# First attention: inputs and normalised outputs turned in 32x32 squares on VectorE instead of by TensorE

## The chip, the cores and the metric

One core of one Trainium2 chip runs the whole program. The metric is the device time in microseconds. The kernel before takes 1017.32 us, the median of three runs (1017.08 to 1018.11).

## The reference, cut to what matters

Two layers. Layer 0: causal attention with 16 heads of 16 columns on 4 x 512 x 256 inputs, rotary turn of the first 4 columns, output projection; then the residual and a layer normalisation; then a "wave" part that gates, mixes and normalises. Layer 1: linear attention and six MLP blocks. The kernel works in fp32, split into a high and a low part for TensorE (`x = x_h + x_l`, three products for one). The change touches layer 0's attention and what hands its result on:

```python
qkv = jnp.einsum('bsh,hf->bsf', hidden_states, w_qkv) + b_qkv
...
scores = jnp.einsum('bhqd,bhkd->bhqk', q, k)
scores = jnp.where(causal, scores, jnp.float32(-jnp.inf).astype(scores.dtype))
probs = jax.nn.softmax(scores, axis=-1)
attn = jnp.einsum('bhqk,bhkd->bhqd', probs, v)
...
return jnp.einsum('bsh,hf->bsf', attn, w_out) + b_out
```

Three things must be turned (token rows to columns) for a product over the hidden dimension: the input of each batch for the projection to q, k and v ("x_T"), the attention's outputs for the output projection ("att_T"), and the normalised rows for the gates of the wave part ("next_T").

## The kernel before, in words

`attention0` handles one batch per entry: `entry(0, "first")`, two of kind "loop", `entry(3, "last")`. An entry has 8 pairs of heads (p) with 4 tiles (r) each: 32 slots (p, r). All engines run the same list of slots, each its own queue in order, tied by semaphores. A slot on TensorE is a score product of two heads (`score_pass`, L849), a product for the row maxima of the pair after next (`max_pass`, L838), often a value product (`value_pass`, L862), and one use of PSUM bank 5 ("work") from the table `WORK_AT`: "stack" (turn the stacked heads, L892), "project" (L885), "out" (L901), and the three kinds of turn (`x_T`, `att_T`, `next_T`, all at L957: four transposes of 128 x 128 for one half c of the columns). Work for batch i+1 (x_T, stack, project) and for batch i-1 (att_T, out, next_T) is woven into entry i. The fourth batch's outputs and normalised rows are turned behind the entries.

ScalarE computes the exponentials (L710), copies PSUM to the heads (`copy_k` L697, `copy_q` L703), rounds the stack (`stack_high`, L689, L691), copies the outputs (L742) and rounds each turned half to its high part (`high`: L678 for x_T, L680 att_T, L682 next_T). VectorE takes the maxima (L1126), the rows of maxima (L1140), adds biases, subtracts the low parts of the turned halves (`low`, L1163), and normalises (`layernorm_steps`, two small steps in each slot from (4, 0) on; the last of them, L167, writes xn at (5, 1)). GpSimd masks the diagonal (`select`, L594), turns by the rotary angles (`rotate`), subtracts the low parts of the stack (L600, L602), adds biases to the residual (L621) and keeps rows (L614). SyncE moves the rows of maxima (`max_row`, L530, two DMAs) and loads each batch's input (L538) as soon as x_T of the one before is split. The score product of slot (p, 0) waits for the row of maxima of its pair; each score product waits for the first exponential of the slot before; each max product for VectorE's maxima of the slot before; a value product for the mask of two slots before. Some filler products (`keep_busy`, L966) stand at (0, 2) and at the places of `KEEP_AT`.

Behind the entries the first waits of the next part are in `gate_product` (L1427, four for each batch) and `gate_function` (L1435). The last stage of the program already turns its rows by squares (L2566, L1687).

Of the kernel before, what the change touches and what calls it, by code (L numbers as in the profile page):

```python
# [25 lines left out]
P = 128  # L26
# [172 lines left out]
def build(nc, A, out):  # L199
# [3 lines left out]
    with top:  # L203
# [78 lines left out]
WORK_AT = ((0, 0, "stack", (1, 0)), (0, 1, "x_T", 0), (0, 2, "stack", (1, 1)),  # L282
           (1, 0, "stack", (1, 2)), (1, 1, "x_T", 1), (1, 3, "stack", (1, 3)),
# [4 lines left out]
           (6, 0, "project", (3, 0)), (6, 1, "project", (3, 1)), (6, 2, "next_T", 0),  # L288
           (7, 0, "project", (3, 2)), (7, 1, "next_T", 1), (7, 3, "project", (3, 3)))
# [14 lines left out]
PREVIOUS = ("att_T", "out", "next_T")  # L304

LOW_FIRST = ((0, 2), (2, 1))
# [13 lines left out]
def work_table(when):  # L320

    table = {}
    for p, r, kind, arg in WORK_AT:
        if kind in PREVIOUS:
            used = when != "first"
        else:
            used = when != "last" if kind == "x_T" else of_entry(when, arg[0])
        if used:
            table[p, r] = (kind, arg)
# [46 lines left out]
def attention0(nc, A, g, top):  # L376
# [21 lines left out]
    s = g.first = sems(top, nc, "ident_in rope_in const_in first_T first_p first_v first_s first_copied qkv_in0 qkv_in1 out_in wsplit_h wsplit_l g_wout const_v mask_v x_in xres_in g_res g_ones "  # L398
# [3 lines left out]
             "v_bias v_matrix a_split v_split a_gate_h v_gate_l p_gate a_gate p_tail v_tail a_c")  # L402
    wqkv_h = put(nc, "wqkv_h", g.early, 0, [KC, 3 * D], F32R)
# [78 lines left out]
    def _(sp):  # L482
# [68 lines left out]

        max_row(-1, "before", 0)
        entries(sp, entry)

    @block.gpsimd
    def _(pool):
# [60 lines left out]

        def residual_bias(b, t):
# [6 lines left out]
        def entry(i, when):  # L625
            table = work_table(when)
            for p in range(PAIRS):
                for r in range(RT):
                    if (p, r) in LOW_AT and of_entry(when, LOW_AT[p, r][0]):
                        stack_low(i, *LOW_AT[p, r])  # L630
                    select(i, p, r)
                    kind, arg = table.get((p, r), (None, None))
# [25 lines left out]
        entries(pool, entry)  # L658
        for t in range(RT):
            keep(B - 1, t)  # L660

    @block.scalar
    def _(act):
# [10 lines left out]
        def high(i, when, kind, arg):  # L674

            act.wait_ge(s["p_work"], WORK.number(i, when, (kind, arg)))
            if kind == "x_T":
                act.activation(x_h[:, arg, :], work, ACT.Copy).then_inc(s["a_xT"], 1)  # L678
            elif kind == "att_T":
                act.activation(att_h[:, arg, :], work, ACT.Copy).then_inc(s["a_attT"], 1)  # L680
            else:
# [2150 lines left out]
```

## Time and profile before

| | |
|---|---|
| median of three runs | 1017.32 us |
| profiled execution, its time | 1017.09 us |
| span of its trace | 1015.0 us |
| mean granted TensorE clock | 0.991 |
| prologue of the first attention | 0 to 28.5 us |
| entries of the first attention | 28.5 to 298 us |
| gates and wave part | 298 to about 430 us |
| busy over the span: TensorE, VectorE, ScalarE, GpSimd | 96%, 75%, 60%, 35% |

PE is TensorE's matmul queue, PEld its weight loads, DVE VectorE, ACT ScalarE, POOL GpSimd, SP SyncE. The chain of work that ended last goes mostly through TensorE's products of the last stage; the change is made long before these. A row of the timeline has the start in us, the duration in us, engine, line, operation, output and inputs with their shapes, and a count where like instructions are merged; in brackets is the idle time before it and what ended that.

### The profile page before, as it was taken

The numbers are of one execution on the slowest core, as the hardware profiler recorded it, in microseconds if no ns is written. First come the engines' busy times: TensorE is split into PE (matmuls) and PEld (weight loads), VectorE is DVE, ScalarE is ACT, GpSimd is POOL, SyncE is SP. The second block draws the span as 40 slices with busy tenths as digits, with TensorE's granted clock in tenths as the row PEclk, the third lists the DMA queues.
The fourth block names the chain that finished last, engine by engine and source line by source line (L and its number), as shares of the span: only waits on it lengthen the run. The fifth ranks groups of instructions, "written<-read, shape, count | busy, mean of one in ns | idle before, by whom it ended". The sixth has DMA issues, their size and how long they took to land.

```text
span 1015.0 us, 18314 instructions
## 1 busy us (share of the span) xinstructions
PE 970.5 (96%) x6498; PEld 806.6 (79%) x6498; DVE 756.8 (75%) x2083; ACT 609.3 (60%) x1177; POOL 360.3 (35%) x646
## 2 busy tenths in 40 slices
PE   8899999998989898999999999999999999999997
PEld 6555555555758798787899999999999999999897
DVE  6677787866656778967767787888778788687874
ACT  5566667655358774645745566665566665566660
POOL 5454374552131374443832222223222232222410
PEclk9999999998999999999999999999999999999999
DMA  7000000013020001032010221220112022121201
GB/s 260 22 2 22 2 23 22 24 43 104 22 89 1 4 2 42 1 104 63 32 53 23 73 67 27 63 64 26 52 45 67 22 64 63 32 62 33 62 32 54
DMA packets 54834, 47.41 MB, mean 47 GB/s; under 512 B 6900, under 2 KB 52184, under 8 KB 54744
## 3 DMA queue, kind: packets, MB, share of 16 engines
q1 hardware_dynamic: 50328, 41.65, 13.5%
q10 hardware_dynamic: 4416, 4.59, 1.5%
q8 instruction: 52, 0.85, 0.4%
q14 instruction: 38, 0.31, 0.1%
HBM read 31.40 MB, written 4.20 MB: 35 GB/s over the span
## 4 chain that ended last, share of the span: by engine, by line
PE 54%; DVE 5%; POOL 2%; issue 1%; ACT 1%; DVEq 0%; POOLq 0%; ACTq 0%
PE ps L1970 24%; PE ps L1987 24%; PE ps L1868 2%; DVE ln_stats L2388 1%; PE ps L2000 1%; PE ps L1919 1%; POOL hs L1765 1%; DVE xT_l L2522 0%; POOL x_b L1765 0%; PE ps L1882 0%; DVE amp L2424 0%; PE ps L1897 0%; DVE G_l L2528 0%; PE ps L1910 0%; POOL x_a L1795 0%
## 5 line engine op out<-in xcount | busy, mean ns | idle before, releaser
L2224 ACT ACTIVATE G<-ps,bias_col 128x512 f32<-128x512 f32 x192 | 135.7, 707 | 156.5 <-PE ps L1970 148.1
L1987 PE MATMUL ps<-w_l,G_h 128*128 128x256 f32 x736 | 203.8, 277 | 0.0
L1987 PE MATMUL ps<-w_h,G_l 128*128 128x256 f32 x736 | 203.8, 277 | 0.0
L1987 PE MATMUL ps<-w_h,G_h 128*128 128x256 f32 x736 | 203.7, 277 | 0.0
L2528 DVE TENSOR_TENSOR G_l<-G,G_h 128x512 fp32r<-128x512 f32 x192 | 164.2, 856 | 48.2 <-ACT G_h L2225 48.2
L1795 POOL TENSOR_TENSOR x_a<-xn,mlp_g 128x1024 f32<-128x1024 f32 x20 | 56.2, 2811 | 326.5 <-DVE xn L2554 326.5
L710 ACT ACTIVATE probs<-ps 128x512 f32<-128x512 f32 (+3 forms) x256 | 98.3, 441 | 97.1 <-PE ps L849 96.3
L1970 PE MATMUL ps<-xT_h,w_h 128*128 128x512 f32 x384 | 150.3, 391 | 0.7 <-DVE xT_l L2522 0.4
L1970 PE MATMUL ps<-xT_h,w_l 128*128 128x512 f32 x384 | 149.6, 390 | 0.0
L1970 PE MATMUL ps<-xT_l,w_h 128*128 128x512 f32 x384 | 149.5, 389 | 0.0
L1126 DVE CUSTOM_DVE_ANT_0 ps<-ps,q_mask 128x128 f32<-128x128 f32 (+3 forms) x256 | 120.7, 512 | 28.7 <-PE ps L838 28.3
L1987 PEld LDWEIGHTS ps<-w_h,G_h 128*128 128x128 f32 x736 | 138.4, 188 | 0.9
L1987 PEld LDWEIGHTS ps<-w_l,G_h 128*128 128x128 f32 x736 | 138.2, 188 | 1.0
L1987 PEld LDWEIGHTS ps<-w_h,G_l 128*128 128x128 f32 x736 | 138.2, 188 | 0.0
L2225 ACT ACTIVATE G_h<-ps,bias_col 128x512 fp32r<-128x512 f32 x192 | 135.3, 705 | 0.0
L594 POOL TENSOR_SCALAR_AFFINE_SELECT probs<-probs 128x256 f32<-128x256 f32 x128 | 53.0, 415 | 99.0 <-ACT probs L710 98.3
L1970 PEld LDWEIGHTS ps<-xT_h,w_h 128*128 128x128 f32 x384 | 72.1, 188 | 15.3 <-issue 0.6
L1970 PEld LDWEIGHTS ps<-xT_h,w_l 128*128 128x128 f32 x384 | 72.1, 188 | 15.2
L1970 PEld LDWEIGHTS ps<-xT_l,w_h 128*128 128x128 f32 x384 | 72.1, 188 | 14.1
L2542 DVE TENSOR_TENSOR rsum<-ps,x_a 128x1024 f32<-128x1024 f32 x23 | 28.2, 1225 | 68.3 <-PE ps L1987 68.3
L838 PE MATMUL ps<-heads_T 64*128 64x128 f32 (+3 forms) x256 | 56.0, 350 | 5.9 <-DVE top_score L1126 5.8
L849 PE MATMUL ps<-heads_T 64*128 64x512 f32 (+3 forms) x256 | 54.3, 419 | 5.2 <-ACT probs L710 3.0
(329 smaller groups left out, 2101.3 us busy)
## 6 DMA issues: line engine op xcount, KB each, us to landing
w_raw<-L_ffn_W_T SPq DMA_DIRECT2D x12, 1024.0 KB, 5.4
landed<-squares SPq DMA_DIRECT2D x320, 32.0 KB, 1.9
hs<-L_attn_hidden_states SPq DMA_DIRECT2D x8, 512.0 KB, 3.9
x_kept<-hs SPq DMA_DIRECT2D x4, 512.0 KB, 4.3
w_raw<-x_kept SPq DMA_DIRECT2D x2, 1024.0 KB, 6.0
out<-xn SPq DMA_DIRECT2D x3, 512.0 KB, 2.8
w_raw<-L_ffn_ent_w_T SPq DMA_DIRECT2D x1, 1024.0 KB, 9.1
w_raw<-L_ffn_ent_pw SPq DMA_DIRECT2D x1, 1024.0 KB, 11.3
```

Of the source, the lines that this page charges most:

```text
L594: pool.affine_select(diagonal, diagonal, [[0, 2], [1, P]], ALU.is_ge, 0.0, base=0, channel_multiplier=-1).then_inc(s["g_sel"], 1)
L710: act.activation(probs[:, p % 2, o, OFF[j]:OFF[j] + COLS[j]], ps[:, score_bank(r, o), 0:COLS[j]], ACT.Exp).then_inc(s["a_exp"], 1)
L838: pe.matmul(ps[:, o, 0:(t + 1) * P], heads_T[rows, p // UP, 0, p % UP, t * P:(t + 1) * P], heads_T[rows, p // UP, 1, p % UP, 0:(t + 1) * P ...
L849: pe.matmul(ps[:, score_bank(r, o), 0:COLS[j]], heads_T[rows, p // UP, 1, p % UP, j * P:(j + 1) * P], heads_T[rows, p // UP, 0, p % UP, j ...
L1126: v.tensor_tensor_reduce(ps[:, o, 0:(t + 1) * P], ps[:, o, 0:(t + 1) * P], q_mask[:, S - (t + 1) * P:S], 1.0, MASKED, ALU.add, ALU.max, to ...
L1795: pool.tensor_tensor(g.x_a[:, rows, :], xn[:, b % 2, :, :], bcast(g.mlp_g[:, i, :], 1, [P, RT, D]), ALU.mult).then_inc(feed["g_mul"], 1)
L1970: mm = pe.matmul(ps[:, hidden_bank(i, n), :], w[:, c, f * P:(f + 1) * P], x[:, b, c, :], start=(k == 0), stop=(k == 5))
L1987: mm = pe.matmul(ps[:, 4 + t // 2, (t % 2) * D:(t % 2 + 1) * D], x[b % 2][f][:, t * P:(t + 1) * P], w2_chunk(w, f), start=(k == 0), stop=( ...
L2224: act.activation(G32[n % 4], bank, ACT.Gelu, bias=bias)
L2225: act.activation(G_h[b % 2][f], bank, ACT.Gelu, bias=bias).then_inc(feed["a_g"], 1)
L2528: v.tensor_tensor(G_l[b % 2][f], G32[n % 4], G_h[b % 2][f].bitcast(F32), ALU.subtract).then_inc(feed["v_gl"], 1)
L2542: v.tensor_tensor(g.rsum[:, :, :], ps[:, 4:6, :].rearrange("p a (b c) -> p (a b) c", c=D), g.x_a[:, b * RT:(b + 1) * RT, :], ALU.add).then ...
```

## The change

Inputs. Each batch is loaded in four quarters of 32 partitions (`load_squares`), so laid out that VectorE's transpose of 32 x 32 squares (`x_turn`, four instructions of 128 x 256 at slots (0, 0), (0, 1), (0, 2), (1, 0)) gives the turned input in SBUF, `x_turned`, which lies in the place of x_l. ScalarE rounds it at (0, 3) and (1, 2), GpSimd subtracts the low part at (1, 0) and (1, 3). The first project product of an entry waits for GpSimd. Batch 0 is turned as before, in the prologue; the load of batch 1 is now issued before the first row of maxima, those of batches 2 and 3 at p = 2 to 5 of entries 0 and 1.

Normalised rows. VectorE transposes the squares of xn behind the normalisation (four instructions of 128 x 256 from slot (5, 2) on, `g.squares`), SyncE moves 16 pieces of squares to `g.landed` at p = 6, 7 and p = 0, 1 of the next entry, ScalarE rounds at (3, 1) and (3, 3) of the entry after that and GpSimd subtracts at (3, 2) and (4, 0). Batch 2's go behind the entries. The first gate product of batches 0 to 2 waits for it. Fillers and all else stay.

```diff
-WORK_AT = ((0, 0, "stack", (1, 0)), (0, 1, "x_T", 0), (0, 2, "stack", (1, 1)),
-           (1, 0, "stack", (1, 2)), (1, 1, "x_T", 1), (1, 3, "stack", (1, 3)),
+WORK_AT = ((0, 0, "stack", (1, 0)), (0, 2, "stack", (1, 1)),
+           (1, 0, "stack", (1, 2)), (1, 3, "stack", (1, 3)),
...
-           (6, 0, "project", (3, 0)), (6, 1, "project", (3, 1)), (6, 2, "next_T", 0),
-           (7, 0, "project", (3, 2)), (7, 1, "next_T", 1), (7, 3, "project", (3, 3)))
+           (6, 0, "project", (3, 0)), (6, 1, "project", (3, 1)),
+           (7, 0, "project", (3, 2)), (7, 3, "project", (3, 3)))
...
-LOW_FIRST = ((0, 2), (2, 1))
+LOW_FIRST = ((2, 1),)
+
+X_TURN_AT = ((0, 0), (0, 1), (0, 2), (1, 0))
+X_HIGH_AT = ((0, 3), (1, 2))
+X_LOW_AT = ((1, 0), (1, 3))
+X_LOAD_AT = (2, 3, 4, 5)
+NEXT_HIGH_AT = ((3, 1), (3, 3))
+NEXT_LOW_AT = ((3, 2), (4, 0))
...
+    SQ, Q = 32, P // 32
+    x_squares = x_in.rearrange("p t d -> p (t d)").rearrange("p (c n r) -> p c n r", c=KC, r=SQ)
+    x_turned = put(nc, "x_turned", g.early, 16 * D, [KC, S // SQ, SQ])
...
         def entry(i, when):
-            if when != "last":
-
-                sp.wait_ge(s["v_xT"], i + 1)
-                sp.dma_start(x_in, x_dram[:, i + 1, :, :]).then_inc(s["x_in"], 16)
             for p in range(PAIRS):
                 if p < PAIRS - 1 or when != "last":
                     max_row(i, when, p + 1)
+                if p in X_LOAD_AT and i + 2 < B:
+                    if p == X_LOAD_AT[0]:
+                        sp.wait_ge(s["v_xturn"], 4 * (i + 1))
+                    load_squares(i + 2, X_LOAD_AT.index(p))
+                if when != "first" and p >= PAIRS - 2:
+                    if p == PAIRS - 2:
+                        sp.wait_ge(s["v_squares"], i)
+                    move_squares(i - 1, p - PAIRS + 2)
+                if i >= 2 and p < 2:
+                    move_squares(i - 2, p + 2)
...
+        def load_squares(b, j):
+
+            rows = A["L0_attn_hidden_states"][b].rearrange("(n t) (c j r) -> j t c n r", t=SQ, c=KC, j=Q)
+            sp.dma_start(x_squares[j * SQ:(j + 1) * SQ, :, :, :], rows[j]).then_inc(s["x_in"], 16)
+
+        def move_squares(b, to):
+
+            for of in range(Q):
+                sp.dma_start(g.landed[to * SQ:(to + 1) * SQ, b, :, :].rearrange("p c (q f t) -> p c q f t", q=RT, f=Q)[:, :, :, of, :],
+                             g.squares[of * SQ:(of + 1) * SQ, b, to, :, :, :]).then_inc(s["moved"], 16)
+
+        sp.wait_ge(s["v_xT"], 1)
+        for j in range(Q):
+            load_squares(1, j)
         max_row(-1, "before", 0)
         entries(sp, entry)
+        for to in (2, 3):
+            move_squares(B - 2, to)
...
+        def x_low(i, c):
+
+            pool.wait_ge(s["a_xT"], KC * (i + 1) + c + 1)
+            pool.tensor_tensor(x_l[:, c, :], x_turned[:, c, :, :].rearrange("p n t -> p (n t)"),
+                               x_h[:, c, :].bitcast(F32), ALU.subtract).then_inc(s["g_xlow"], 1)
+
+        def next_low(b, c):
+
+            pool.wait_ge(s["a_nT"], KC * b + c + 1)
+            pool.tensor_tensor(g.xT_l[:, b, c, :], g.landed[:, b, c, :], g.xT_h[:, b, c, :].bitcast(F32),
+                               ALU.subtract).then_inc(s["g_nlow"], 1)
...
+        def x_high(i, c):
+
+            act.wait_ge(s["v_xturn"], 4 * i + 2 * c + 2)
+            act.activation(x_h[:, c, :], x_turned[:, c, :, :].rearrange("p n t -> p (n t)"), ACT.Copy
+                           ).then_inc(s["a_xT"], 1)
+
+        def next_high(b, c):
+
+            act.wait_ge(s["moved"], 16 * Q * Q * (b + 1))
+            act.activation(g.xT_h[:, b, c, :], g.landed[:, b, c, :], ACT.Copy).then_inc(s["a_nT"], 1)
...
             if kind == "project":
+                if arg == (2, 0):
+                    pe.wait_ge(s["g_xlow"], KC * (i + 1))
                 mm = project(work, *arg)
...
+        def x_turn(i, part):
+
+            if part == 0:
+                v.wait_ge(s["x_in"], 16 + 64 * (i + 1))
+            c, n = part // 2, part % 2 * (S // SQ // 2)
+            v.transpose(x_turned[:, c, n:n + S // SQ // 2, :], x_squares[:, c, n:n + S // SQ // 2, :]
+                        ).then_inc(s["v_xturn"], 1)
...
+            yield
+            v.wait_ge(s["v_norm"], i + 1)
+            for k in range(RT):
+                ins = v.transpose(g.squares[:, i - 1, :, :, k, :].rearrange("p j c s -> p c j s"),
+                                  xn[:, 0, k, :].rearrange("p (c j s) -> p c j s", c=KC, j=Q))
+                if k == RT - 1:
+                    ins.then_inc(s["v_squares"], 1)
+                yield
+                yield
...
@@ -1420,6 +1488,8 @@
     b, w, m = n // 4, n // 2 % 2, n % 2
     if n >= 4:
         pe.wait_ge(g.first["a_gate"], n - 3)
+    if n % 4 == 0 and b < B - 1:
+        pe.wait_ge(g.first["g_nlow"], KC * (b + 1))
```

## Rows read from the trace of the kernel before

**Rows 1.** Busy time in stretches: us, PE, PEld, DVE, ACT, POOL, clock, DMA share, GB/s.

```profile
30.00:298.00 268.00, 247.89 (x1735) 156.10 (x1737) 194.45 (x722) 159.02 (x406) 121.53 (x330) 0.97 0.12 35
200.00:205.00 5.00, 5.00 (x34) 2.87 (x34) 2.11 (x9) 2.21 (x4) 1.68 (x4) 0.66 0.02 3
```

**Rows 2.** Line 957's transposes of inputs and normalised rows: ns min/median/max, first and last start.

```profile
L957 PE MATMUL ps<-ident,hs x24: 272/273/448, 33.8 to 164.4; 128*128 128x128 f32 x24
L957 PE MATMUL ps<-ident,xn x24: 272/273/329, 144.0 to 295.3; 128*128 128x128 f32 x24
```

**Rows 3.** Timeline around slot (0, 1) of the second entry: TensorE, then ScalarE.

```profile
94.42 0.44 PE L849 MATMUL ps<-heads_T 64*128 64x384 f32 x2
...
94.09 0.44 ACT L710 ACTIVATE probs<-ps 128x128 f32<-128x128 f32 x2
```

**Rows 4.** Timeline around slot (6, 2) of the second entry: TensorE, then ScalarE.

```profile
144.05 0.66 PE L957 MATMUL ps<-ident,xn 128*128 128x128 f32 x4
144.63 0.38 PE L849 MATMUL ps<-heads_T 64*128 64x256 f32 x2
...
147.29 0.44 PE L885 MATMUL ps<-wqkv_h,x_h 128*128 128x384 f32 x1 [0.22 <-DVE xT_l L1163]
...
144.56 0.60 ACT L742 ACTIVATE out_T<-ps 128x512 f32<-128x512 f32 x1
145.04 0.62 ACT L682 ACTIVATE xT_h<-ps 128x512 fp32r<-128x512 f32 x1
145.51 0.69 ACT L710 ACTIVATE probs<-ps 128x256 f32<-128x256 f32 x2
```

**Rows 5.** Timeline around slot (7, 1) of the second entry: TensorE, then ScalarE.

```profile
149.85 0.45 PE L849 MATMUL ps<-heads_T 64*128 64x384 f32 x2
...
148.91 0.45 ACT L710 ACTIVATE probs<-ps 128x128 f32<-128x128 f32 x2 [0.97 <-PE ps L849]
```

**Rows 6.** Prices: moves and transposes of squares by tile; GpSimd's timeline; VectorE's groups.

```profile
L1687 SPq DMA_DIRECT2D landed<-squares x320: 585/597/1794, 532.2 to 958.8; - x160
L2566 DVE STREAM_TRANSPOSE squares<-xn x80: 391/416/440, 528.6 to 948.7; 128x256 f32<-128x256 f32 x80
...
20.50 1.30 POOL L651 TENSOR_TENSOR wout_l<-probs,wout_h 128x512 fp32r<-128x512 f32 x1
...
L1163 DVE TENSOR_TENSOR x_l<-ps,x_h 128x512 fp32r<-128x512 f32 x6 | 4.1, 689 | 2.9 <-ACT x_h L678 2.9
```

**Rows 7.** Timeline of the first rows of maxima: SyncE's issues, then TensorE.

```profile
21.18 0.43 SPq L522 DMA_DIRECT2D last_b<-L_ffn_ln_b  x1
26.11 1.34 SPq L530 DMA_DIRECT2D heads_T<-neg_rows  x2
...
28.54 0.50 PE L849 MATMUL ps<-heads_T 64*128 64x512 f32 x2 [0.28 <-DMA heads_T<-neg_rows]
```

**Rows 8.** Busy time in stretches with DMA: prologue, squares moves, an input load.

```profile
24.00:25.00 1.00, 1.00 (x5) 0.57 (x4) 1.00 (x4) 0.00 (x0) 0.92 (x5) 1.00 0.62 216
535.00:537.00 2.00, 2.00 (x20) 2.00 (x19) 0.00 (x0) 0.00 (x0) 0.00 (x0) 1.00 0.21 56
28.00:31.00 3.00, 1.85 (x7) 0.67 (x6) 1.90 (x7) 1.08 (x2) 0.96 (x2) 1.00 0.54 175
```

**Rows 9.** Timeline at slots (5, 2) and (5, 3) of the second entry: TensorE, then VectorE.

```profile
136.35 0.50 PE L838 MATMUL ps<-heads_T 64*128 64x512 f32 x1 [0.94 <-DVE top_score L1126]
...
133.70 2.07 DVE L167 TENSOR_SCALAR xn<-rsum,ln_mv,ln_y 128x256 f32<-128x256 f32 x4
```

**Rows 10.** Timeline at slots (1, 2) and (1, 3) of the second entry: GpSimd, then TensorE.

```profile
102.99 0.46 POOL L600 TENSOR_TENSOR q_stack<-qkv,q_stack 128x128 fp32r<-128x128 f32 x1 [0.49 <-ACT k_stack L691]
103.40 0.47 POOL L602 TENSOR_TENSOR k_stack<-qkv,k_stack 128x128 fp32r<-128x128 f32 x1
...
104.39 0.28 PE L892 MATMUL ps<-ident_r,k_stack 128*128 128x128 f32 x1
```

**Rows 11.** Timeline of ScalarE behind the entries, the fifth and sixth gate function.

```profile
312.81 1.27 ACT L1435 ACTIVATE amp<-ps,bias_col 128x512 f32<-128x512 f32 x2
```

More of the change, by code:

```diff
@@ L326, in work_table @@
         else:
-            used = when != "last" if kind == "x_T" else of_entry(when, arg[0])
+            used = of_entry(when, arg[0])
         if used:
@@ L631, in entry @@
                     select(i, p, r)
+                    if when != "last" and (p, r) in X_LOW_AT:
+                        x_low(i, X_LOW_AT.index((p, r)))
+                    if i >= 2 and (p, r) in NEXT_LOW_AT:
+                        next_low(i - 2, NEXT_LOW_AT.index((p, r)))
                     kind, arg = table.get((p, r), (None, None))
@@ L658, in _ @@
         entries(pool, entry)
+        for c in range(KC):
+            next_low(B - 2, c)
         for t in range(RT):
@@ L759, in entry @@
                         copy_q(i, when, *arg)
-                    elif kind in ("x_T", "att_T", "next_T"):
+                    elif kind == "att_T":
                         high(i, when, kind, arg)
+                    if when != "last" and (p, r) in X_HIGH_AT:
+                        x_high(i, X_HIGH_AT.index((p, r)))
+                    if i >= 2 and (p, r) in NEXT_HIGH_AT:
+                        next_high(i - 2, NEXT_HIGH_AT.index((p, r)))
                     if (p, r) in HIGH_AT and of_entry(when, HIGH_AT[p, r][0]):
@@ L804, in _ @@
             act.activation(att_h[:, c, :], ps[:, c, :], ACT.Copy).then_inc(s["a_attT"], 1)
+        for c in range(KC):
+            next_high(B - 2, c)
         act.wait_ge(s["v_split"], STAGES)
@@ L945, in use_work @@
             else:
-                if kind == "x_T":
-                    pe.wait_ge(s["x_in"], 16 * (i + 2))
-                    src = x_in
-                elif kind == "att_T":
-                    pe.wait_ge(s["ex_read"], EXCHANGE.number(i, when, ("group", -1)) + 1)
-                    src = att
-                else:
-                    pe.wait_ge(s["v_norm"], i + 1)
-                    src = xn[:, 0, :, :]
+                pe.wait_ge(s["ex_read"], EXCHANGE.number(i, when, ("group", -1)) + 1)
                 for t in range(RT):
-                    mm = pe.transpose(work[:, t * P:(t + 1) * P], src[:, t, arg * P:(arg + 1) * P], ident[:, :])
+                    mm = pe.transpose(work[:, t * P:(t + 1) * P], att[:, t, arg * P:(arg + 1) * P], ident[:, :])
             mm.then_inc(s["p_work"], 1)
@@ L1269, in normalise @@
                                        (s["g_x1"], i))
+            if when == "after":
+                return
+            yield
[7 more added lines that the diff above has]
+                yield
         PREPARE_AT = ((1, 2), (1, 3), (2, 0), (2, 1), (2, 2), (2, 3), (3, 2), (3, 3), (4, 0), (5, 1), (5, 3), (6, 1),
@@ L1280, in entry @@
                 kind, arg = table.get(slots[n - 1], (None, None)) if n else (None, None)
-                turned = kind in ("x_T", "att_T", "next_T")
+                turned = kind == "att_T"
                 if turned and (p, r) in LOW_FIRST:
@@ L1296, in entry @@
                 kind, arg = table.get((p, r), (None, None))
+                if when != "last" and (p, r) in X_TURN_AT:
+                    x_turn(i, X_TURN_AT.index((p, r)))
                 if when == "last" and (p, r) in PREPARE_AT:
```

27 lines of the change are left out of this document (7 added, 20 removed).

## The prediction

> **What bounds the kernel now.** I read the page first, then the busy time by stage, then single slots. Only the first attention is edited, and what follows it is edited in one wait. In its entries, 30 to 298 us, TensorE's records cover 247.9 of 268 us [rows 1], so time taken from TensorE there looks like time gained. But a matmul record overlaps the next one, and "busy" hides waits: the question for each removed group is what the next score product was waiting for. I call a pair of heads p and a tile r of it "slot (p, r)", as the code does; an entry has 32 slots. The score product of a slot starts when TensorE is free and when the exponential of the previous slot's first head is out. So I compare, at each removed group, the start of the next score product with the end of that exponential.
>
> **What is removed.** Twelve groups of four transposes go: six of the inputs ("hs") and six of the normalised rows ("xn"), 24 transposes of each with a median of 0.273 us [rows 2]. Four of them overlap: from the first of a group to the next product TensorE's order takes 0.58 us, from 144.05 to 144.63 [rows 4]. With them go twelve subtractions on VectorE at 0.69 us [rows 6]. The twelve rounding copies on ScalarE (0.6 us) stay, but at other slots.
>
> Input turns, slot (0, 1). In the second entry ScalarE writes the two 128-column exponentials from 94.09, 0.28 us each, so the first is out at 94.37; the next score product starts at 94.42 [rows 3]. The transposes before it hide wholly behind ScalarE, which is still working through the copies of the stack. Removing them gains 0.05 us. Slot (1, 1) looks the same (copies, then exponential), so I take 0.1 us an entry for the second and third entry. In the first entry the group runs at the lower clock (0.448 us at most in place of 0.273) [rows 2] and I take 0.5. Sum: 0.7 us.
>
> Turns of the normalised rows, slots (6, 2) and (7, 1). At (6, 2) the score product starts at 144.63, but what counts is ScalarE: it copies the outputs (144.56), copies the turned rows (145.04, 0.62) and only then reaches the next exponential at 145.51, for all of which slot (7, 0) waits [rows 4]. Without the copy it starts some 0.5 earlier; that is the gain of this slot (TensorE's 0.58 is not added to it). At (7, 0) the project product waits 0.22 us for VectorE's subtraction [rows 4]: gone too. At (7, 1) the exponential is out at 148.91 + 0.28 = 149.19 and the score product starts at 149.85 [rows 5]: the full 0.6 is TensorE's. Together 1.3 us in the second entry and the same in the third; in the last entry the project product is missing and ScalarE is nearer behind, so I take 0.8. Sum: 3.4 us. Bounds for all twelve groups: nothing, and 12 x 0.6 = 7.2 plus waits.
>
> **What is added, and what covers it.** VectorE gets 12 transposes of 256 columns for the inputs and 12 for the rows. The trace has that form in the last stage, 0.42 us each [rows 6]: 24 x 0.42 = 10.0 us added against 12 x 0.69 = 8.3 removed. VectorE is busy 194 of 268 us [rows 1], so the sum of +1.7 is free; the place is what matters. The rows' transposes come one a slot from (5, 2) on, just behind the normalisation, which already holds VectorE 2.07 us and lets TensorE wait 0.94 us for a maximum [rows 9]. The first new transpose stands behind the maximum that TensorE waits for, so this stall doesn't grow; the next maximum slips 0.4 us, and its taker is a slot away. I take 0, bound 0.4 x 3.
>
> GpSimd gets 12 subtractions of 512 columns. Exactly that form stands in the prologue at 1.30 us; VectorE does it in 0.69 [rows 6]. 15.6 us on an engine busy 121.5 of 268 [rows 1] are affordable, but its queue is in order. Behind the new subtraction of slot (1, 0) wait the masks of slot (1, 1), then the low parts of the stack. In the second entry these end at 103.87 and TensorE uses them at 104.39 [rows 10]: 0.5 us of slack against 1.3 us. But GpSimd also waits for ScalarE on the way there, 0.49 us in the last of the two slots [rows 10]; with as much in the slot before, 1.3 - 1.0 = 0.3 us arrives and is covered. VectorE can also be held while GpSimd works: four normalisation steps that GpSimd overlaps took 2.07 us [rows 9]. I charge 0.3 us in all; bound 0 to 2.
>
> The Trainium skill speaks against this part: "GPSIMD Engine Reference", section 4.1 Engine selection, sends elementwise work with two inputs to VectorE, GpSimd being about twice as slow. The rows agree with 1.30 to 0.69 us; by the rule alone the move would be a loss of 12 x 0.6 = 7 us, which holds only if GpSimd's queue were the path, and the rows above say it isn't.
>
> SyncE. The 48 moves of squares (16 for each batch, 0.6 us each to issue as in the last stage [rows 6]) stand behind the row of maxima of slots (6, 1), (7, 1) and (0, 1), (1, 1), and the next such row is due four slots, some 8 us, later, against 4 x 0.6 = 2.4. Hidden; ScalarE takes the result at slot (3, 1) or after the last entry. In the last entry the 16 moves take 9.6 us to issue, from about its slot (6, 1) on; ScalarE asks after the entry, four gate functions and the copies of the attention's outputs. The loads of the next inputs are the same: free, except the first.
>
> The first load, start of the first entry. SyncE now issues four quarter loads of batch 1 at about 21.6, before the row of maxima of pair 0, which it issued at 26.11 and for which TensorE waited until 28.54 [rows 7]. The queue works off older loads until about 24.6 [rows 8]. The new load reads 4,096 runs of 128 bytes instead of 512 of 1 KB. Price of a run: moves in runs of 512 bytes ran at 56 GB/s for a share of 0.21, that is 267 GB/s at full share or 31 ns a run for one of 16 engines; 1 KB runs at 175 for 0.54, 324 GB/s, 51 ns [rows 8]. A line through both gives 17 ns for 128 bytes: 4,096 x 17 / 16 = 4.3 us, to 28.9. The row of maxima would then land about 1.1 us after, near 30.0 instead of 28.5: +1.4 us. Lower end: by bytes alone 1.6 us, no delay. Upper end: a run costs as much as one of 512 bytes, 7.9 us, delay 5. I take the line, since both its points are runs of the same queue.
>
> "DMA: Bandwidth & Descriptors" in the Trainium skill, section Why small descriptors are slow, gives about 3 cycles of overhead on each packet; with its fabric clock that makes an estimate of 8 ns for 128 bytes, 2.1 us for the load, and no delay: the sum would be 1.4 us lower. No run so far shows such a load.
>
> The tail. ScalarE copies the last turned rows (2 x 0.6) ahead of the sines; the gate functions behind them start 1.1 us later than 312.81, and TensorE's ninth gate product needs the first of them [rows 11]; products for three others lie between. I charge 0.2; bound 0 to 1.1.
>
> The clock. The mean granted clock of the entries is 0.97, so 0.03 x 268 = 8 us of full clock are missing. One such stretch lies in 200 to 205 us: mean 0.66, so 0.34 x 5 = 1.7 us missing [rows 1], 1.7 us lost at most, and some five like it in all, at 1.2 instead of 2.4 GHz. Ahead of this one TensorE had waited for VectorE, as in rows 9. The change takes work from TensorE exactly where it often waits, in p = 0, 1 and 6, 7. I charge half a unit, +0.6; bounds -2 to +5.
>
> **Sum**, against the profiled execution's 1017.09 us (span 1015.0 and 2.1 around it; the median of the three runs is 1017.32): -0.7 - 3.4 + 0 + 0.3 + 1.4 + 0.2 + 0.6 = -1.6, rounded 1015.4 us. A difference of 0.2%, 2 us, is about the least that can be told here.
>
> **Rivals.** (1) TensorE's order is the path throughout, as its 247.9 of 268 us suggest. Then all twelve groups count: -7.2, less 1.0 for start and tail: 1010.9. Against it: rows 3. (2) The gain goes to the clock: two or three more stretches at 1.2 GHz at up to 1.7 us, in place of the half: 1017 to 1018, no change. For it: the removed products are in the stretches with the most waits. (3) Slower: the 128-byte load holds the row of maxima. It decides from 8 us of load on (31 ns a run): +5 in place of +1.4, and with a longer idle TensorE a further stretch of low clock, 1.2: 1020. (4) GpSimd's subtraction comes late for the stack at (1, 3) and for slot (4, 0): from a price of 1.8 us on (contention with VectorE), 0.5 us at each of 12 places: +5, 1020. (5) It doesn't do what it says, the moves being visible in front of ScalarE's copies: each late move set costs 2 to 3 us; three sets, 1021.
>
> **How the numbers follow.** Chances: the forecast 0.42 (1013.5 to 1017.2, of it 0.22 below the mark for faster), (1) 0.19, (2) 0.18, (3) 0.12, (4) 0.06, (5) 0.03. Faster: 0.22 + 0.19 + 0.02 of (4), the prices being milder = 0.43. Slower: 0.12 + 0.04 + 0.03 + 0.01 of (2) = 0.20. Same: the rest, 0.37. The range reaches from rival (1) to just under (3): 1010.5 to 1019.5. Cases of both signs hold most of it; the forecast's own range is 1013.5 to 1017.2.
>
> **What would show it.** Start: the idle time of the first score product ahead of slot (0, 0), and its releaser; right if it starts near 30.0, wrong if at 28.5 or 33. Slot (0, 1) to (0, 2): spacing unchanged within 0.1 us in the second entry. (6, 2) to (7, 2): shorter by 1.1 to 1.3 us. GpSimd: its groups of 12 subtractions near 1.3 us, with no wait of TensorE for k_stack beyond those of before. Moves: no wait of ScalarE at (3, 1). The clock: the count of stretches at 1.2 GHz between 30 and 298 us. The prediction is wrong if the input slots shorten, if waits for VectorE's maxima grow, or if the count changes by two or more.

## The result, and the profile after

The changed kernel takes 1029.39 us, the median of five runs (1023.68 to 1031.13), against 1017.58 (1017.08 to 1018.11) for the kernel before: a ratio of 1.0107, 95% interval 1.0091 to 1.0123. The forecast was 1015.4 us, with a range up to 1019.5: the change is slower by 1.1%, outside the range.

Two lines of the page of after: busy time over the span of 1027.5 us, and the granted clock in 40 slices.

```profile
PE 979.6 (95%) x6450; PEld 809.2 (79%) x6450; DVE 758.2 (74%) x2095; ACT 609.5 (59%) x1177; POOL 376.3 (37%) x658
...
PEclk9699998989999999999999999999999999999999
```

The mean granted clock is 0.973 over the whole program (0.991 before). So the first question was where it is low. In the busy time by stretch the last three columns are clock, DMA share and GB/s; these are the stretches of the entries in which the clock stands at 1.2 GHz, in the trace of after:

```profile
29.70:43.30 13.60, 11.89 (x44) 7.61 (x44) 6.83 (x26) 6.78 (x17) 3.23 (x8) 0.50 0.00 1
46.80:50.20 3.40, 3.40 (x20) 0.90 (x20) 1.32 (x6) 2.11 (x6) 2.13 (x7) 0.50 0.01 1
60.40:63.80 3.40, 3.40 (x16) 2.51 (x19) 1.47 (x7) 0.43 (x2) 0.49 (x3) 0.51 0.01 1
108.20:111.60 3.40, 3.40 (x24) 0.90 (x20) 1.39 (x6) 2.18 (x6) 2.10 (x7) 0.50 0.04 8
145.80:149.20 3.40, 3.40 (x17) 1.74 (x16) 1.26 (x7) 2.01 (x4) 0.41 (x1) 0.50 0.01 2
156.00:166.20 10.20, 10.20 (x42) 6.00 (x42) 5.04 (x20) 3.50 (x10) 4.92 (x13) 0.50 0.12 21
214.00:217.40 3.40, 3.40 (x16) 1.83 (x17) 0.97 (x6) 1.70 (x4) 0.41 (x1) 0.51 0.02 5
224.30:231.10 6.80, 6.80 (x27) 3.72 (x27) 3.37 (x16) 2.62 (x9) 4.36 (x11) 0.50 0.06 11
255.00:261.80 6.80, 6.55 (x27) 5.14 (x27) 5.73 (x21) 2.84 (x6) 1.88 (x3) 0.50 0.01 2
```

and in that of the kernel before (these rows were not shown ahead; [rows 1] had a cut of the second):

```profile
33.80:37.20 3.40, 3.40 (x12) 2.26 (x13) 2.10 (x8) 2.17 (x7) 1.64 (x4) 0.50 0.01 4
201.00:204.40 3.40, 3.40 (x20) 1.71 (x19) 1.11 (x7) 2.21 (x4) 0.68 (x2) 0.51 0.02 5
224.90:228.30 3.40, 3.40 (x12) 2.33 (x12) 1.66 (x7) 0.99 (x4) 1.70 (x5) 0.51 0.26 77
242.00:248.80 6.80, 5.35 (x25) 4.20 (x24) 5.25 (x21) 2.10 (x5) 1.20 (x3) 0.50 0.02 7
```

54.4 us at the low level against 17.0: 16 pieces of 3.4 us ("units" below) against 5. A slot's start is its first score product (L849 before, L911 after). The last one begins at 296.82 us before and 309.24 after, 12.42 later, and from there to the end both take the same (718 us). Of the 12.42, 1.42 are there at the first score product, 11.51 in slots that touch a low unit in either trace, and -0.51 in all others. Eleven units more for 11.5 us.

Slots without a low unit agree within 0.06 us, but for those next to the edits. GpSimd's subtractions took what was read from rows, with one exception, which comes up again at the end (a mean of 1452 ns for the rows' six, since one of them took 2.27 us):

```profile
L659 POOL TENSOR_TENSOR xT_l<-landed,xT_h 128x512 fp32r<-128x512 f32 x6 | 8.7, 1452 | 10.1 <-ACT xT_h L738 10.1
L653 POOL TENSOR_TENSOR x_l<-x_turned,x_h 128x512 fp32r<-128x512 f32 x6 | 7.7, 1280 | 0.0
```

The start, in the timelines of after: SyncE's issues, then TensorE.

```profile
20.98 6.48 SPq L571 DMA_DIRECT2D hs<-L_attn_hidden_states  x4
27.50 1.36 SPq L540 DMA_DIRECT2D heads_T<-neg_rows  x2
...
29.96 0.80 PE L911 MATMUL ps<-heads_T 64*128 64x512 f32 x2 [1.68 <-DMA heads_T<-neg_rows]
```

SyncE is held for 6.48 us issuing the four quarter loads, while the DMA engines are busy with older loads (a share of 0.86 to 1.31 in each microsecond from 20 to 26 us). The row of maxima goes out at 27.50 instead of 26.11 [rows 7]. From there to the first score product it is 2.46 us, against 2.43 before, so the whole delay lies in the issue. TensorE waits 1.68 us instead of 0.28, and 13.6 us at the low clock follow. Before, a single piece of 3.4 us followed, 5 us after the first score product.

### The profile page after: what moved, and what is told of

It reads as the page before. It is cut to its first block, busy times and chain, and to the rows that moved or that the text cites. A ratio compares the mean times of both kernels' runs of the same rounds, so it can differ in the third digit from the quotient of the medians.

```text
span 1027.5 us, 18289 instructions
## 1 busy us (share of the span) xinstructions
PE 979.6 (95%) x6450; PEld 809.2 (79%) x6450; DVE 758.2 (74%) x2095; ACT 609.5 (59%) x1177; POOL 376.3 (37%) x658
## 4 chain that ended last, share of the span: by engine, by line
PE 53%; DVE 5%; POOL 2%; issue 1%; ACT 1%; DVEq 0%; POOLq 0%; ACTq 0%
PE ps L2040 24%; PE ps L2057 23%; PE ps L1938 2%; DVE ln_stats L2458 1%; PE ps L2070 1%; PE ps L1989 1%; POOL hs L1835 1%; DVE xT_l L2592 0%; POOL x_b L1835 0%; PE ps L1952 0%; DVE amp L2494 0%; PE ps L1967 0%; DVE G_l L2598 0%; PE ps L1980 0%; PE ps L1889 0%
## 5 line engine op out<-in xcount | busy, mean ns | idle before, releaser
L900 PE MATMUL ps<-heads_T 64*128 64x128 f32 (+3 forms) x256 | 59.8, 373 | 6.4 <-DVE top_score L1181 6.2
L911 PE MATMUL ps<-heads_T 64*128 64x512 f32 (+3 forms) x256 | 56.6, 438 | 7.1 <-ACT probs L766 5.2
```

Source lines behind the costliest of these rows:

```text
L900: pe.matmul(ps[:, o, 0:(t + 1) * P], heads_T[rows, p // UP, 0, p % UP, t * P:(t + 1) * P], heads_T[rows, p // UP, 1, p % UP, 0:(t + 1) * P ...
L911: pe.matmul(ps[:, score_bank(r, o), 0:COLS[j]], heads_T[rows, p // UP, 1, p % UP, j * P:(j + 1) * P], heads_T[rows, p // UP, 0, p % UP, j ...
```

## Experiments

All runs are compared with the kernel before, run beside them (104 runs in all, median 1017.66); the kernels have 4 to 12 runs each. "Clock" is the mean over a kernel's runs of the mean granted clock. The last column is explained below the table.

| kernel | median us | ratio (95%) | clock | us at equal clock |
|---|---|---|---|---|
| before | 1017.66 | | 0.990 | 1010.2 |
| after | 1029.39 | 1.0107 (1.0091 to 1.0123) | 0.975 | 1010.1 |
| e1 turns unread | 1016.90 | 0.9995 (0.9984 to 1.0005) | 0.990 | 1009.8 |
| e2 late load | 1021.48 | 1.0048 (1.0029 to 1.0067) | 0.980 | 1008.5 |
| e3 both | 1015.57 | 0.9982 (0.9972 to 0.9991) | 0.991 | 1009.1 |
| e4 before, no turns | 1030.61 | 1.0133 (1.0113 to 1.0152) | 0.971 | 1009.0 |
| e5 rows' slots | 1023.51 | 1.0038 (1.0018 to 1.0058) | 0.983 | 1009.4 |
| e6 input slots | 1022.02 | 1.0041 (1.0026 to 1.0057) | 0.981 | 1008.7 |
| e7 fillers | 1018.45 | 1.0004 (0.9990 to 1.0018) | 0.990 | 1010.8 |
| e8 + wait at (5, 3) | 1016.27 | 0.9980 (0.9971 to 0.9990) | 0.992 | 1010.3 |
| e9 + start | 1013.74 | 0.9966 (0.9955 to 0.9978) | 0.995 | 1010.3 |
| e10 early squares | 1021.30 | 1.0037 (1.0021 to 1.0054) | 0.982 | 1007.6 |
| e11 all | 1014.06 | 0.9969 (0.9956 to 0.9982) | 0.994 | 1010.1 |
| e12 before, filled | 1012.06 | 0.9958 (0.9943 to 0.9974) | 0.996 | 1009.7 |
| e13 no input turns | 1022.08 | 1.0052 (1.0028 to 1.0075) | 0.983 | 1009.8 |
| e14 no row turns | 1023.43 | 1.0063 (1.0038 to 1.0087) | 0.979 | 1008.7 |
| e15 no turns, filled | 1016.46 | 1.0002 (0.9984 to 1.0021) | 0.988 | 1008.7 |
| e16 changed, filled | 1015.86 | 0.9985 (0.9969 to 1.0001) | 0.990 | 1008.4 |

The span times one minus the clock is the full-clock time a run misses: 26 us after, 10.6 before. Over the 140 runs of e1 to e16, each taken against the mean of its own kernel, a missing microsecond costs 0.70 us (0.03 either way). A unit misses 0.5 x 3.4 = 1.7 us, so 1.2 us a unit. The last column is the mean of time minus 0.70 x missing. The clock is given to 0.001, so a single run's figure is good to 0.35 us only. That the 0.70 found among runs of one kernel also holds between kernels is an assumption: where two kernels miss 10 us more or less, an error of 0.1 in it shifts their difference by 1 us.

The count of low units comes from one traced run of each kernel, and not always from a typical one: that of e3 took 1018.73 us, the longest of its ten, and that of e12 1014.73, the longest of its five.

**e1, e2, e3: the work put back, the load put back.** The edit of e1, at the four slots where turns stood:

```diff
+                    if (p, r) in UNREAD_AT and when != ("last" if p < 2 else "first"):
+                        wait(pe, s["work_read"], ...)
+                        for t in range(RT):
+                            pe.transpose(work[:, t * P:(t + 1) * P], ident[:, :], ident[:, :])
```

and of e2; e3 has both:

```diff
-        sp.wait_ge(s["v_xT"], 1)
-        for j in range(Q):
-            load_squares(1, j)
         max_row(-1, "before", 0)
+        sp.wait_ge(s["v_xT"], 1)
+        for j in range(Q):
+            load_squares(1, j)
```

> The changed kernel, with the removed TensorE work put back as work that nobody reads: at slots (0, 1), (1, 1), (6, 2) and (7, 1), in the entries where inputs or normalised rows were turned before, four transposes of the identity go into the work bank. Everything else is as after the change. Theory C (the loss is TensorE's clock, which falls because work is gone from those slots): the trace of after has 16 stretch units of 3.41 us at 1.2 GHz before 310 us, that of before 5; four of the 16 stand at the start and stay, the others fall back to 4 or 5, so 8 or 9 in all, each unit about 1.2 us; with the turns' own 2 to 3 us back the time is 1029.4 - 8 x 1.2 + 3 = 1022 us, between 1020 and 1025. Theory S (everything follows from the late start, which shifts the schedule against the clock): the count stays near 16 and the time is 1030 to 1032. Theory W (new waits on VectorE, GpSimd or moves): 1030 to 1032 too, with the count of low units falling.

> The changed kernel, with the four quarter loads of batch 1 issued behind the first row of maxima, as the load stood before the change. Theory C: the start goes back to 28.5 us (-1.4) and the four low units at the start go (about -4 us), the later ones stay: 12 units, 1024 us, between 1022 and 1026. Theory S: with the start back, all of the later units go as well: about 5 units and 1014 to 1015 us. If the load is not what delays the start: 1029 us, start at 30.0.

> Both edits together: late load of batch 1, and unread transposes in the four slots. Theory C: TensorE has the work of before at the places of before, the count is 4 to 6 units and the time that of before, 1016 to 1018 us. Theory S: the same as the late load alone plus the transposes, 1016 to 1018; the two theories part in the other runs. Theory W: 1024 us or more, with 5 units.

e1 came to 1016.90 (3 us below what theory C gave) with 5 units in its trace (8 or 9 forecast), e2 to 1021.48 with 9 (12 forecast), e3 to 1015.57 with 7 (4 to 6 forecast). Work that nobody reads makes the changed kernel 12 us faster, so theory W falls. Theory S falls as a full account: with the start back at 28.86 us, e2 still has 9 units and 4 us of loss. But the late start is part of the cause. Moving the load back, which brings the start 1.1 us earlier, brings 7.9 us in the medians (5.8 in the means). Either repair undoes most of the loss, and with the turns' work in place the late start costs no more than itself: e1 is 1.3 us behind e3.

**e4: the removal alone.**

```diff
-                if kind == "x_T":
-                    pe.wait_ge(s["x_in"], 16 * (i + 2))
-                    src = x_in
+                if kind in ("x_T", "next_T"):
+                    pe.wait_ge(*((s["x_in"], 16 * (i + 2)) if kind == "x_T" else (s["v_norm"], i + 1)))
+                    pe.sem_inc(s["p_work"], 1)
+                    return
```

> The kernel before, with the 48 transposes of inputs and normalised rows left out and nothing added; ScalarE's copies and VectorE's subtractions of the turned halves stay and read what is left in the bank, so the batches after the first are computed from other data. Nothing is moved and the start is as before. Theory C: the removal alone lowers the clock: 5 units become 10 to 14, at 1.2 us each, less 2 to 3 us of turns: 1021 to 1026 us. Theories S and W: the count stays at 5 and the time falls by the turns, 1014 to 1015 us.

Measured: 1030.61, the slowest of all, and 4.6 us above the upper end of what theory C gave (1021 to 1026). The kernel before with 48 transposes less, and nothing else in its program touched, loses 13 us; its later batches are computed from other data, while those of e1 and e2 are the right ones. Its clock in 40 slices, from the page:

```profile
PEclk9899988988989999999999999999999999999999
```

and its busy time over the entries, with a clock of 0.91 in them where [rows 1] had 0.97:

```profile
28.50:310.00 281.50, 258.04 (x1707) 157.97 (x1708) 195.02 (x724) 160.31 (x409) 122.34 (x330) 0.91 0.12 34
```

Its trace has 15 units before 310 us, against 5. That shows the cause: take the transposes away and the granted clock falls (e4), give TensorE other work in their place and it comes back (e1). What the removal is worth at equal clock, e4 can't tell: 1009.0 against 1010.2, but its four runs leave 0.8 us of uncertainty. The same kernel with fillers in two waits (e15, below), whose clock is close to that of before, comes to 1008.7, 1.5 us less, where theories S and W had 2 to 3 us. The clock takes this back many times over.

**e5, e6: one pair of slots each,** on top of e2, by leaving entries out of UNREAD_AT.

> Changed kernel with the late load of batch 1 (1021.5 us) and unread transposes only in the slots of the normalised rows, (6, 2) and (7, 1) of entries 1 to 3. The late load alone left 5 of its 9 low units at (6, 3) to (7, 3) of entries 1 and 2. If the clock is lost where the rows' turns stood, this gives nearly all that both pairs of slots gave: 1016 to 1017 us and about 6 units. If the input slots matter as much: 1018.5. If it is the input slots alone: 1021 to 1022.

> Changed kernel with the late load and unread transposes only in the slots of the inputs, (0, 1) and (1, 1) of entries 0 to 2. If the clock is lost at the rows' slots: 1020 to 1021 us, with low units at (6, 3) to (7, 3) of entries 1 and 2. If both matter alike: 1018.5. If the input slots alone: 1016 us.

1023.51 and 1022.02 against e2's 1021.48: neither brought anything that shows (their means are less than 1 us below e2's, which is itself good to 1 us), though both together (e3) bring 6 us. Their traces have 11 units each, against 9 in e2's and 7 in e3's. Each run by itself looks like the case in which the other pair carries the clock, so none of the cases I wrote down covers both.

**e7, e8, e9: fillers.** e7 puts `keep_busy(work, count)` in place of the unread transposes (2, 4, 2, 2 products); e8 adds three before the max product of (5, 3), e9 four more at (0, 0):

```diff
                         score_pass(i, p, r)
+                    else:
+                        keep_busy(outputs, 4)
+                    if (p, r) in FILL_BEFORE_MAX and when != "first":
+                        wait(pe, s["work_read"], ...)
+                        keep_busy(work, FILL_BEFORE_MAX[p, r])
```

> Changed kernel with the late load and, in the four slots, filler products (fp32r, 128 x 512) in place of the unread transposes: 2 at (0, 1), 4 at (1, 1), 2 at (6, 2), 2 at (7, 1). If what counts for the clock is that TensorE has work there, whatever its form, the time is that of the transposes or a little less, 1014.5 to 1016 us, since two fillers take about 0.43 us against 0.58 for four transposes; 6 to 7 units. If the form matters (an fp32 transpose keeps TensorE busy otherwise than an fp32r product), 1018 to 1021.

> As the filler run, with 3 more fillers in the 0.93 us in which TensorE waits for VectorE's maximum behind the normalisation, between the score and the max product of slot (5, 3), entries 1 to 3. By the clock theory the low unit that the kernel before shows at 201 us and the likes of it go, each worth 1.2 us, and the fillers cost nothing since they lie in a wait: 1 to 2 us under the filler run, 1013 to 1014 us. If the clock there doesn't hang on this wait: no change, or up to 0.3 us more.

> The kernel with fillers in the four slots and at (5, 3) (1016.3 us), with 4 fillers more between the first score product and the first max product of slot (0, 0), where TensorE waits 0.93 us for VectorE. Clock theory: its trace has three low units from 30.9 us on, right behind this wait; they fall to one or none, each worth 1.2 us: 1013.5 to 1015 us. If the low clock at the start comes from the wait for the row of maxima (up to 28.9 us) and not from this one: 1016 us, unchanged.

(Entries are counted from 0, so entry 1 is the second.) e7 came to 1018.45, its clock (0.990) about that of e3 (0.991), but its runs spread from 1015.04 to 1020.24 and its time at equal clock is 1.7 us longer. The expectation of 1014.5 to 1016 failed: the four products at (1, 1) lengthen that slot by 0.43 us in entries 1 and 2, where I had read a free wait of 0.91. That is half of the 1.7. The fillers in real waits brought about what was forecast for them: 2.2 us for those at (5, 3) (1 to 2 forecast, though from e7's higher level the time is 1016.27 and not 1013 to 1014), 2.5 us for those at the start.

**e10: VectorE's transposes two at a time,** on top of e2:

```diff
                     ins.then_inc(s["v_squares"], 1)
                 yield
-                yield
```

> The late-load kernel (1021.5 us), with VectorE's transposes of the normalised rows two at a time, so that the last of them stands at about slot (6, 0) and none just ahead of the maxima of slot (6, 2). Theory V: the transpose ahead of the maxima is why the spacing from (6, 3) to (7, 0) grew by 0.37 us and TensorE's max product at (6, 3) waits 0.27; with the transposes out of the way the spacing of entries 1 and 2 is back at 1.72 us, and each entry gains 0.4. In all 1 us at equal clock: the time less 0.7 of the full-clock microseconds that the mean granted clock says are missing falls from 1008.5 to 1007.5; the plain time is 1018 to 1023, by the clock. If something else lengthens the slot: spacing 2.09 and 1008.5 as before.

The slot from (6, 3) to (7, 0), 0.37 us longer than before in e2, is 0.12 longer here, and the time at equal clock falls from 1008.5 to 1007.6, good to 0.35 us. Theory V holds for two thirds of the 0.37.

**e11, e12: everything together, and the kernel before with two fillers.** e12 is the kernel before with `keep_busy(outputs, 4)` at slot (0, 0) and `keep_busy(work, 3)` at (5, 3) of entries 1 to 3.

> All repairs together: late load, fillers in the four slots, in the wait of (5, 3) and at the start, and VectorE's row transposes two at a time. If the gains add: 1010.2 (what all kernels so far come to when 0.7 of the missing full-clock time is taken off, for the kernel before) less 1.7 for the late load less 1 for VectorE, plus 5 for 7 us of missing clock: 1012.5 to 1014 us, 0.4% under the kernel before. If VectorE's part is nothing: 1014 to 1015.5. If clock falls elsewhere instead: 1016 to 1017.

> The kernel before with nothing but fillers in two of its waits: 4 at the first max product of slot (0, 0) and 3 between the score and max product of slot (5, 3), entries 1 to 3. Clock theory: its units at 33.8 and 201 us go, 5 units become 3: 1015 to 1016 us. If the kernel before stands at a floor that fillers don't move: 1017.5 us.

e11 came to 1014.06, no faster than e9: the case in which VectorE's part is nothing, so that e10's 0.9 us at equal clock isn't seen again here. e12 came to 1012.06, 0.42% under the kernel before, the fastest median of all, with none of the change in it, and 3 us below what I expected. In its traced run the unit at 201 us is gone and one near 35 us is still there. TensorE's timeline at slots (5, 2) and (5, 3) of the second entry, first the score product of before that precedes the wait of [rows 9]:

```profile
135.03 0.39 PE L849 MATMUL ps<-heads_T 64*128 64x256 f32 x2
```

and below it the same stretch of e12:

```profile
136.34 0.38 PE L849 MATMUL ps<-heads_T 64*128 64x256 f32 x2
136.65 0.98 PE L966 MATMUL ps<-wout_h 128*128 128x512 f32 x3
137.67 1.01 PE L838 MATMUL ps<-heads_T 64*128 64x512 f32 x2
```

The three fillers lie where TensorE had waited: the max product starts 1.33 us after the score product, against 136.35 - 135.03 = 1.32 before.

**e13 to e16: one kind of turn removed, and fillers without the turns.** e13 and e14 are e4 for "x_T" and for "next_T" alone; e15 is e4 and e16 is e2 with the two groups of fillers of e12.

> The kernel before, with the 24 transposes of the inputs alone left out (batches after the first are computed from what lies in the bank); those of the normalised rows stay. Both left out gave 1030.6 us against 1017.6. If the two removals add and weigh alike: 1024 us. If one removal is enough to lose the clock at many places (two repairs of one pair of slots each brought nothing): 1027 to 1030. If the input slots don't matter: 1017 to 1018.

> The kernel before, with the 24 transposes of the normalised rows alone left out (their high and low parts are taken from what lies in the bank). If the removals add and weigh alike: 1024 us. If one is enough: 1027 to 1030. If only the input slots matter: 1017 or, by the turns' time, 1016.

> The kernel before without any of the 48 transposes (1030.6 us), with the fillers that brought the kernel before to 1012.1 us: 4 at the first max product of slot (0, 0), 3 in the wait of slot (5, 3) in entries 1 to 3. If the fillers of two waits hold the clock whatever else is removed: 1010 to 1012 us, and the removal is worth 1 us. If the removed work has to be replaced where it stood: some 4 of 13 units come back, 1024 to 1027 us.

> The changed kernel with the late load (1021.5 us) and the same two groups of fillers, none in the four slots of the removed turns. If the fillers of two waits hold the clock: 1011 to 1013 us. If the removed work has to be replaced where it stood: 1017 to 1020 us, against 1013.7 with fillers in the four slots as well.

Alone, the inputs' turns cost 4.4 us to remove and the rows' 5.8 (1022.08 and 1023.43, under the 1024 of the case in which both weigh alike); both together cost 13.0. So each removal loses clock by itself, with 9 and 10 units in the traces. Whether they add can't be told: the sum of 10.2 is good to 3 us, the 13.0 to 2. The fillers in two waits bring back 14 us, all of e4's loss and 1 more, and 5.6 us in e2. That lies in neither of the two cases I had written down for each: it is more than I expected of work that stands elsewhere, but neither kernel reaches e12's 1012.06. Their clocks are 0.988 and 0.990 against 0.996.

e16 has a stretch from 106.7 to 212.3 us at full clock, so its second entry can be set beside the same one of before slot by slot from (2, 0) on. Around slot (7, 1), TensorE and VectorE of before:

```profile
149.13 0.42 DVE L1126 CUSTOM_DVE_ANT_0 ps<-ps,q_mask 128x256 f32<-128x256 f32 x1
149.27 0.66 PE L957 MATMUL ps<-ident,xn 128*128 128x128 f32 x4
...
149.47 0.46 DVE L1126 CUSTOM_DVE_ANT_0 ps<-ps,q_mask 128x256 f32<-128x256 f32 x1
...
150.13 0.35 PE L838 MATMUL ps<-heads_T 64*128 64x384 f32 x2
...
150.41 1.07 PE L862 MATMUL ps<-probs,val 128*32 128x512 f32 x8
...
151.41 0.39 PE L849 MATMUL ps<-heads_T 64*128 64x256 f32 x2
```

and of e16:

```profile
151.32 0.42 DVE L1186 CUSTOM_DVE_ANT_0 ps<-ps,q_mask 128x256 f32<-128x256 f32 x1
151.43 0.44 PE L911 MATMUL ps<-heads_T 64*128 64x384 f32 x2
...
151.66 0.47 DVE L1186 CUSTOM_DVE_ANT_0 ps<-ps,q_mask 128x256 f32<-128x256 f32 x1
...
151.85 0.82 PE L900 MATMUL ps<-heads_T 64*128 64x384 f32 x2
...
152.60 1.07 PE L924 MATMUL ps<-probs,val 128*32 128x512 f32 x8
...
153.60 0.39 PE L911 MATMUL ps<-heads_T 64*128 64x256 f32 x2
```

Without the turn the score product follows the maxima 0.61 us sooner (0.11 after VectorE's first maximum begins, against 0.72 [rows 5]). But the pair of max products then takes 0.82 instead of 0.35 us, since the second waits for VectorE's second maximum, and the next score product is 2.17 us behind instead of 1.56. All 0.61 are given back within one slot. e15 shows the same with none of VectorE's new work and with ScalarE's copies at their old places: there the score product of (7, 2) comes 0.49 us sooner, and the next slot is 0.50 longer.

## Why the prediction was wrong, step by step

**The clock** is the step that failed: +0.6 with bounds of -2 to +5 us. The runs: after misses 26.1 us of full clock against 10.6, and 15.5 x 0.70 = 10.9 us, all of the loss (10.8 us in the means, 11.8 in the medians). The mechanism was named ("takes work from TensorE exactly where it often waits"), and rival (2) was built on it, with two or three stretches more. There were eleven. I sized it by what the clock had cost so far, five units, and not by how many places were near to losing it: with 12 groups removed and a longer wait at the start there was room for far more than five, and nothing in the trace bounded it from above. In hindsight the runs give 0.7 us for each group removed (e13), 1.0 (e14) and 1.1 (e4), so a bound of one unit for every group, 12 x 1.2 = 14 us, would have held. The charge itself had no source either: half of a unit at 1.7 us is 0.85, not 0.6.

On the direction the trace agrees with a page: the Trainium skill, "TensorE: Matmul & The Clock Gate", Terms, puts the penalty of throttled time at its length times one minus the ratio, which is 0.5 here, 1.7 us a unit and 19 us for eleven. The runs show 1.2. That TensorE's queue is not always the path while its clock is low would explain the rest; no run here tests it.

**The first load**, +1.4 us: the start came at 29.96 against 30.0 forecast. The size was right by luck, and the mechanism wrong. I had the row of maxima land late behind 4.3 us of transfers; in fact SyncE could not issue it. One of the four loads held SyncE's queue for 4.0 us, and the row went out at 27.50. In e2, with the queues empty, the same four are issued from 27.82 on in 2.85 us and each lands 2.9 us after its issue, so the last is there about 5 us after the first issue. The transfer itself, in the busy time of e2 (the last three columns as above):

```profile
29.30:32.70 3.40, 2.22 (x11) 1.29 (x9) 2.21 (x11) 1.08 (x2) 0.41 (x1) 0.83 0.98 154
```

That is 0.98 x 16 x 3.4 us for 4,096 runs, 13 ns a run and 3.3 us in all. The line through two prices had 17 (worked out rightly it gives 16), and the estimate from the Trainium skill, "DMA: Bandwidth & Descriptors", 8 ns and 2.1 us: the one is too high, the other too low, and neither has the time that SyncE is held. What I missed wholly is what the wait does: 13.6 us at the low clock behind it. In e1, with the same load and the turns back, it was 10.2.

**Input turns**, -0.7: in e16 entries 1 and 2 gain 0.18 and 0.22 us from (0, 2) to (0, 3), and nothing from (0, 1) to (0, 2), as forecast. About 0.4 for the two, against 0.2. The 0.5 of the first entry can't be read: its slots run partly at the low clock, and not at the same places, in the two traces.

**Turns of the normalised rows**, -3.4 with 1.3 an entry, is the second step that failed. Slot by slot in e16's second entry: -0.29 at (6, 2), +0.36 at (6, 3), -0.14 at (7, 0), -0.61 at (7, 1), +0.61 at (7, 2), -0.18 at (7, 3): 0.25 us in all. The score products do come sooner, by 0.3 and 0.6 us. e15, which removes the turns alone, has 0.21 us in the same entry, so most of the gain is missing before any work is put on another engine. In the last entry 0.65 us are gained against 0.8. Together that is 1.15 us against 3.4. ScalarE's copy, which I had taken for the path at (6, 2), was not: it stays in e15, and the slots come out alike. VectorE's maxima stand right behind the score products, and I had asked only what the next score product waits for, not what the max product behind it waits for.

**VectorE's additions**, 0 with a bound of 0.4 x 3: the transpose ahead of the maxima of (6, 2) is 0.25 of the +0.36 at (6, 3), by e10, two times (entries 1 and 2). So some 0.5 us, and e10 as a whole gains 0.9 at equal clock.

**GpSimd**, +0.3: its subtractions take 1.28 and 1.29 us in the median (forecast 1.30), and TensorE waits for k_stack twice, 0.9 us in all, as often and as long as before. But one place pays, the slot (4, 0) of the last entry, 0.21 us longer (5.56 against 5.35; 5.60 in e2 and e16, 5.41 in e15, which has no such subtraction). After, and below it before:

```profile
266.76 1.25 DVE L1303 TENSOR_TENSOR gate_l<-raw_gate,gate_h 128x1024 fp32r<-128x1024 f32 x1
266.90 2.27 POOL L659 TENSOR_TENSOR xT_l<-landed,xT_h 128x512 fp32r<-128x512 f32 x1
...
269.19 1.42 DVE L1306 TENSOR_TENSOR stage_c<-stage_c,x_a 128x1024 f32<-128x1024 f32 x1
...
271.26 3.72 PE L1001 MATMUL ps<-w_raw 128*128 128x256 f32 x16 [0.57 <-DVE rsum L1259]
```

```profile
256.33 1.21 DVE L1251 TENSOR_TENSOR stage_c<-stage_c,x_a 128x1024 f32<-128x1024 f32 x1
...
258.20 3.72 PE L937 MATMUL ps<-w_raw 128*128 128x256 f32 x16 [0.36 <-DVE rsum L1204]
```

The subtraction takes 2.27 us beside VectorE's long one. GpSimd's next mask comes late behind it, at 269.13, and now runs beside VectorE's L1306, which takes 1.42 us where L1251 took 1.21; TensorE's wait grows by as much. e2 has the same, 2.27 and 1.41 us. So 0.2 us against 0.3, and by these rows in the way that was named (VectorE held while GpSimd works). The rule of the Trainium skill weighed there ("GPSIMD Engine Reference", section 4.1) has the right ratio, and its 7 us of loss don't appear. The moves: the profile shows no wait of ScalarE for them. **The tail**, +0.2: the fifth gate function comes at 326.31, 1.08 later than 312.81 [rows 11] plus the shift of 12.42; later ones are late by 0.42 (330.12 against 317.28) and by 0.02 (333.94 against 321.50). Nothing at the end.

Sum at equal clock: forecast -2.2 without the clock, measured -0.1 (1010.1 against 1010.2, good to 0.5); without the late start -1.7 (e2). The slots say the same: +1.4 for the start, -0.4 for the inputs, -1.15 for the rows, +0.2 for GpSimd, 0.05 in all. (The sum in the prediction gives 1015.5, not 1015.4.) Three of the signs listed ahead came out against the forecast. The way from (6, 2) to (7, 2) is 0.68 us shorter in e16, not 1.1 to 1.3, and nearly all of it is given back one slot on. TensorE's waits for VectorE's maxima grew, its weight loads included, from 16.2 to 17.3 us. And the count of stretches went from 5 to 16, which alone outweighs all else.

**Left open.** Why putting back one pair of slots brings nothing when both bring 6 us, why a late start costs so much only where the turns are gone, and why e4 and e2, with the same products on TensorE, differ by 9 us and 0.01 of clock. A kernel's clock also differs from run to run: e2's ten runs go from 1017.67 to 1027.50. Which wait loses the clock in a given run can't be read from these runs.

## What to carry to other kernels

Where a trace already shows stretches at TensorE's low clock, work taken from TensorE may be no gain: ask first at how many places it would have waited anyway, and set the bound at a low stretch for each (0.7 to 1.1 us for each group of four transposes here). A product that nobody reads, put into a wait that is there already, is the cheaper change (0.4% here for five lines). For the gain itself follow the slot one step further than the next product: the engine that answers it (VectorE's maxima here) must have room as well. And an early load costs its issuing engine's time: look at what stands behind it in that queue while older loads are under way.

## What the hardware showed

- Removing 48 transposes of 0.27 us made a kernel 13 us slower, with nothing else in its program changed (e4).
- A microsecond of full clock missing costs 0.70 us here, a 3.4 us stretch at 1.2 GHz 1.2 us.
- Loads in runs of 128 bytes took 13 ns a run on each of 16 DMA engines (e2).
- Beside a VectorE subtraction of 128 x 1024 a GpSimd subtraction took 2.27 us in place of 1.28 (after).
- One DMA issue took 4.01 us on SyncE, in place of 0.7, while older loads were under way. From the trace of after, loads of the inputs' quarters before 30 us:

```profile
L571 SPq DMA_DIRECT2D hs<-L_attn_hidden_states x4: 670/838/4011, 21.0 to 26.8; - x4
```
